# Raw dt as an outer product on TensorE; one more accumulating DMA for the state sums, and the skip term, gate and out-projection of a tile in parts

## The chip, the cores and the metric

One NeuronCore of a Trainium2 chip runs the whole program. The metric is device time in microseconds; of the kernel before there are three timed runs: 2022.76, 2023.56 and 2023.82 us (median 2023.56). Each kernel also has one profiled execution.

## What is computed

One perceiver layer over 64 batches of 32 rows of width 512 (all fp32 unless said): cross attention to 257 keys per batch with 16 heads, then a Mamba block, then a feed-forward net with quantised inputs and weights, each added to its input. The part that the change touches is the Mamba block (1024 inner channels, 16 states):

```
bcd = einsum('ble,ep->blp', x_, x_proj_w)             # B, C and one raw dt per row
dt  = softplus(bcd[..., -1:] * dt_w + dt_b)           # 1024 channels from one number per row
h_t = exp(dt*A) * h_(t-1) + (dt * x_) * B             # scan over the 32 rows of a batch
y   = sum over 16 states (h_t * C) + x_ * D           # D: the skip term
y   = y * silu(z);  out = y @ out_proj_w              # gate and out-projection
```

## The kernel before

The 2048 rows are 16 tiles of 128 rows (4 batches each). Channels lie on the partitions: 8 chunks `c` of 128 channels, so `dt`, `u`, `xs`, `zs`, `xD` are 128 x 8 x 128. PE, ACT, DVE, POOL and SP each run one instruction stream, written out by hand in `schedule` in one common order; semaphores connect them. `interval(ta, tm, to, more)` handles at once tile `ta` in attention, tile `tm = ta-1` in the first part of Mamba and tile `to = ta-2` in its second part. It has four steps, b = 0 to 3, one batch of attention each. Intervals 3 to 14 are one loop; 0, 1, 2 and 15 are written apart, and `tail` finishes the last two tiles. The feed-forward net follows.

What each step does on each engine, around the change:

- PE starts a step with `scores` (L1025, into banks 2 to 5) of a batch, then turns the next batch's context (L958), makes its keys (`kv_keys`, L992, banks 6 and 7, halves j = 0 and 1), transposes the softmax (L1034), makes values (L1003) and weighs them (L1045, bank 4). In b = 0 it also turns the normalised tile (L1092) and makes its first in-projection (L1099); in b = 1 it makes `bcd` (L1126), broadcasts the dt row over the partitions (L1134), makes the gate's in-projection (L1099) and the out-projection of tile `to` (`mamba_out`, L1140, bank 5).
- DVE takes the scores from the banks in four passes (`score_pass`, L1697) for a batch. In b = 0 this is preceded by `x1_write` (L1724), the attention's result; its layer norm (statistics on DVE, L1598 and L1603; rstd on POOL, L1498 to L1503; rows on ACT, L1304) leads to PE's L1092. Between these stand the steps of the state scan: `CHAIN` is a list of (chunk, op) with op 0 the product u*B (L1815), op 1 the scan (L1820), op 2 the product with C (L1826), op 3 the sum over 16 states (`last_sum`, L1792 and L1797). `BEGIN` and `FINISH` say at which place of a step which entries of `CHAIN` stand, for tile `tm` and tile `to`.
- For op 3, POOL's DMA (L1545) first adds states 8 to 15 onto 0 to 7 in memory, for every chunk but the last one (`whole(c)`), for which DVE does this level too (128x1024).
- `mamba_steps` (L1764): DVE makes the raw dt of the 8 chunks from the broadcast row by eight multiply-adds. `mamba_softplus` on ACT: Abs, Exp (both 128x1024), Ln in halves (L1415 to L1420). `mamba_dt` (L1770): DVE makes max(dt, 0) + ln(...) in halves. `mamba_u` (L1782): u = dt*xs in halves. `decays` (L1443): ACT makes exp(dt*A), eight instructions for half a chunk.
- `mamba_gated` (L1896, L1899): DVE adds the skip term `xD` and multiplies with the gate, each over all 8 chunks, in b = 1 after the last sum of tile `to`; then `mamba_u` of tile `tm` may write `u`, and PE's `mamba_out` starts.
- POOL also scales the mask for each batch (L1517) and copies x1 to x2 (`mamba_keep`, L1576, end of b = 3), which `x1_write` of the next interval waits for.

Of the kernel before, what the change touches and what calls it, by code (L numbers as in the profile page):

```python
# [39 lines left out]
def perceiver_kernel(nc, x, ctx_kv, mask, Wq, bq, Wk, bk, Wv, bv, Wo, bo, Win, conv_w, conv_b, Wx,  # L40
# [13 lines left out]
    with ExitStack() as ctx:  # L54
# [35 lines left out]
        chan = sb("chan", [P, 4, IC])  # L90
# [167 lines left out]
        bc_loaded = [sem("b_loaded"), sem("c_loaded")]  # L258
        dt_step = sem("dt_step")
# [4 lines left out]
        hb_added = [sem("hb_added0"), sem("hb_added1")]  # L264
        sum_step = sem("sum_step")
# [64 lines left out]
        DONE = {step: k + 1 for k, step in enumerate(CHAIN)}  # L330
        FINISH = {(0, "a"): range(21, 22), (0, "b"): range(22, 26), (0, "c"): range(26, 28),
                  (1, "a"): range(28, 29), (1, "t"): range(29, 31), (1, "p"): range(31, 32)}
        BEGIN = {(1, "w"): range(0, 1), (1, "d"): range(1, 3), (1, "e"): range(3, 4), (2, "a"): range(4, 5),
# [15 lines left out]
        def tail(part):  # L349
# [31 lines left out]
            part.mamba_steps(LAST)  # L381
# [55 lines left out]
        def schedule(part, engine):  # L437
# [22 lines left out]
            def interval(ta, tm, to, more):  # L460

                here, front, back = ta is not None, tm is not None, to is not None
                for b in range(BT):
# [57 lines left out]
                    if b == 1 and front:  # L521
                        part.rows_load(tm, 0)
                        part.mamba_steps(tm)
# [9 lines left out]
                    if following and b == 0:  # L533
                        part.kv_values(g + 1, 0, range(0, 2))
                    if here:
                        part.normalise(g)
# [21 lines left out]
                    if b == 1 and front:  # L558
                        part.mamba_softplus(tm)
                        part.mamba_gate(tm, keys)  # L560
                        part.mamba_dt(tm)
                    place("b")
# [24 lines left out]
                    if b == 1 and back:  # L587
                        part.mamba_gated(to)
                    if b == 1 and front:
                        part.mamba_u(tm)  # L590
                    if here:
                        part.weigh_values(g, ta, b)
# [38 lines left out]
        class Part:  # L631
# [33 lines left out]
            def weigh_values(self, g, t, b): pass  # L665
# [17 lines left out]
            def mamba_steps(self, t): pass  # L683
            def mamba_softplus(self, t): pass
            def mamba_dt(self, t): pass
            def mamba_u(self, t): pass
# [3 lines left out]
            def mamba_gated(self, t): pass  # L690
# [56 lines left out]
        def whole(c):  # L747
            return c == IC - 1

# [4 lines left out]
        BQKV_DMAS, EARLY_DMAS, OTHER_DMAS = 9, 2, 9  # L754
# [3 lines left out]
        def _(sp):  # L758
# [128 lines left out]
            def rest_of_setup():  # L887
                sp.dma_start(bo_sb[:], bo.partition_broadcast(P)).then_inc(early_loaded, 16)
                sp.dma_start(idb[:], ident_b).then_inc(w_loaded, 16)
                with nc.allow_non_contiguous_dma(reason="small vectors, once"):  # L890
                    sp.dma_start(convw[:], conv_w.rearrange("(c p) o k -> p c (o k)", p=P)).then_inc(w_loaded, 16)
                    for i, v in enumerate((conv_b, dt_w, dt_b, Dskip)):
                        sp.dma_start(chan[:, i, :], v.rearrange("(c p) -> p c", p=P)).then_inc(w_loaded, 16)
                    sp.dma_start(wo_sb[:], Wo.rearrange("(c p) n -> p c n", p=P)).then_inc(wo_loaded, 16)
# [37 lines left out]
        def _(pe):  # L932
# [10 lines left out]
            class Products(Part):  # L943
# [25 lines left out]
                def kv_keys(self, g, b, ta, tm, to, more):  # L969
# [5 lines left out]
                    for j in range(2):  # L975
                        if b == 0 and j == 0 and to is not None:
# [60 lines left out]
                def weigh_values(self, g, t, b):  # L1037
# [1011 lines left out]
```

## Time and profile before

| | us |
|---|---|
| median of 3 timed runs | 2023.56 |
| the profiled execution's own time | 2018.77 |
| its span, first to last instruction | 2017.0 |
| PE busy | 1853.5 (92%) |
| DVE busy | 1851.5 (92%) |
| ACT busy | 1622.9 (80%) |
| POOL busy | 493.6 (24%) |

The page gives the share of each engine over the whole span. In its 40 slices DVE stands at 9 tenths from slice 4 to slice 38, PE nearly so from slice 2 to slice 34. An engine's wait is put down to what released it; idle time is in square brackets in the timelines. Matmul records carry their latency, so the distance from one start to the next says what a group takes.

### The profile page before, as it was taken

Reading aid. Unit: us, or ns where it says so; the run is one execution under the profiler, and the core shown is the slowest. Engines: PE = TensorE matmul, PEld = TensorE weight load, DVE = VectorE, ACT = ScalarE, POOL = GpSimd, SP = SyncE. Lnnn points to the kernel's source line nnn. Section 1 sums busy time; section 2 is a strip of 40 time slices with the busy share of each in tenths; the row PEclk is TensorE's granted clock in tenths of the full one; section 3 lists DMA queues with packets and bytes.
Section 4 is the critical chain, followed back from the end, with each engine's and each line's share of the span. In section 5 each row is a group of like instructions: output and inputs, shape, how many; then the busy total and the mean of one; then the engine's idle time right before and its main releaser. Section 6 shows DMA issues by size and latency. Waiting matters only on the chain. (4 is left out here: it accounts for less than half of the span.)

```text
span 2017.0 us, 43545 instructions
## 1 busy us (share of the span) xinstructions
PE 1853.5 (92%) x14733; PEld 1275.4 (63%) x14748; DVE 1851.5 (92%) x2320; ACT 1622.9 (80%) x4425; POOL 493.6 (24%) x392
## 2 busy tenths in 40 slices
PE   7998998999999999999999999999998999567899
PEld 5576666756575766666676767666666657366444
DVE  1647999999999999999999999999999999999788
ACT  3458888898988889898889788888988888867483
POOL 1001214131414232241413141422314131201013
PEclk9999999999999999999999999999999999789899
DMA  9623333333433333343333334343333333420214
GB/s 300 218 77 95 85 95 85 93 80 85 86 105 74 97 80 75 93 94 90 82 95 80 86 74 115 66 93 87 77 95 85 93 79 91 94 85 11 74 45 143
DMA packets 93456, 189.54 MB, mean 94 GB/s; under 512 B 18768, under 2 KB 39904, under 8 KB 88160
## 3 DMA queue, kind: packets, MB, share of 16 engines
q1 hardware_dynamic: 78448, 133.32, 21.0%
q0 software_dynamic: 14832, 54.01, 14.5%
q8 instruction: 94, 1.54, 0.3%
q14 instruction: 82, 0.67, 0.1%
HBM read 116.12 MB, written 17.18 MB: 66 GB/s over the span
## 5 line engine op out<-in xcount | busy, mean ns | idle before, releaser
L1443 ACT ACTIVATE dA<-dt,A_sb 128x124 f32<-128x124 f32 x2048 | 618.0, 397 | 12.5 <-DVE dt L1770 12.4
L1820 DVE TENSOR_TENSOR_SCAN hb<-dA,hb 128x2048 f32<-128x2048 f32 x118 | 522.4, 4427 | 8.1 <-ACT dA L1443 4.3
L992 PE MATMUL bank<-ctxT,wk_sb 128*128 128x256 f32 x2048 | 466.5, 384 | 30.4 <-ACT Q L1329 19.6
L1003 PE MATMUL bank<-wv_sb,ctxT 128*128 128x512 f32 x1024 | 476.7, 607 | 2.3 <-ACT ctxT L1262 2.3
L992 PEld LDWEIGHTS bank<-ctxT,wk_sb 128*128 128x128 f32 x2048 | 382.1, 191 | 99.7 <-ACT Q L1329 25.3
L1003 PEld LDWEIGHTS bank<-wv_sb,ctxT 128*128 128x128 f32 x1024 | 189.0, 193 | 194.9 <-issue 189.5
L1545 POOL DMA_DIRECT2D hb<-hb x103 | 93.5, 908 | 858.9 <-DVE hb L1826 843.6
L1815 DVE TENSOR_TENSOR hb<-u,BC 128x2048 f32<-128x2048 f32 x118 | 270.4, 2291 | 5.7 <-DVE u L1782 2.6
L1826 DVE TENSOR_TENSOR hb<-hb,BC 128x2048 f32<-128x2048 f32 x117 | 268.9, 2298 | 1.5
L1099 PE MATMUL bank<-xn2T,win_sb 128*128 128x128 f32 x2048 | 239.0, 278 | 0.7 <-ACT xn2T L1358 0.7
L1099 PEld LDWEIGHTS bank<-xn2T,win_sb 128*128 128x128 f32 x2048 | 236.4, 195 | 4.2 <-issue 2.2
L1517 POOL TENSOR_SCALAR maskn<-maskb 128x257 f32<-128x257 f32 x64 | 137.6, 2150 | 260.8 <-DVE soft L1697 258.4
L1299 ACT ACTIVATE Pr<-Pr,soft 128x257 f32<-128x257 f32 x256 | 127.4, 506 | 56.7 <-DVE soft L1697 56.7
L1792 DVE TENSOR_TENSOR hb<-hb 128x512 f32<-128x512 f32 (+2 forms) x248 | 149.6, 603 | 5.0 <-DMA hb<-hb 0.5
L1336 ACT ACTIVATE Pr<-Pr,soft 128x256 f32<-128x256 f32 x256 | 109.0, 503 | 23.6 <-DVE soft L1710 23.6
L1278 ACT ACTIVATE KT<-bank,bqkv 128x256 f32<-128x256 f32 x256 | 105.6, 464 | 26.3 <-PE bank L992 26.2
L1262 ACT ACTIVATE ctxT<-bank,lastT 128x256 f32<-128x256 f32 x256 | 102.5, 479 | 27.8 <-PE bank L958 25.6
L1285 ACT COPY V<-bank 128x512 f32<-128x512 f32 x128 | 74.7, 583 | 58.2 <-PE bank L1003 29.1
L1756 DVE SCALAR_TENSOR_TENSOR xs<-xpad,convw,xs 128x128 f32<-128x128 f32 x384 | 103.7, 347 | 14.9 <-ACT xs L1377 14.4
L1140 PE MATMUL bank<-wout_sb,zs 128*128 128x512 f32 x240 | 106.9, 598 | 0.0
L1034 PE MATMUL bank<-idf,Pr 128*128 128x128 f32 x512 | 79.5, 285 | 29.7 <-ACT Pr L1336 26.7
L1697 DVE CUSTOM_DVE_ANT_0 Pr<-bank,maskn 128x257 f32<-128x257 f32 x256 | 93.1, 421 | 10.8 <-PE bank L1025 10.8
(167 smaller groups left out, 2434.0 us busy)
## 6 DMA issues: line engine op xcount, KB each, us to landing
hb<-hb POOLq DMA_DIRECT2D x103, 512.0 KB, 5.2
ctx_sb<-in_ctx_dram SPq DMA_DIRECT2D x64, 512.0 KB, 4.0
BC<-bcd_dram SPq DMA_DIRECT2D x32, 1024.0 KB, 7.2
maskb<-in_mask_Bx1x1xS_fk_dram SPq DMA_DIRECT2D x64, 128.5 KB, 3.3
wstage<-in_L_ffn_w_dram SPq DMA_DIRECT2D x4, 2048.0 KB, 11.3
x_sb<-in_x_dram SPq DMA_DIRECT2D x16, 256.0 KB, 3.7
win_sb<-in_L_attn_in_proj_w_dram SPq DMA_DIRECT2D x1, 4096.0 KB, 25.1
bo_sb<-bias_dram SPq DMA_DIRECT2D x64, 64.0 KB, 2.0
```

The source lines that it names most:

```text
L992: last = pe.matmul(bank[6 + j][:, (m % 2) * KF:(m % 2 + 1) * KF], wk_sb[:, c, m * P:(m + 1) * P], ctxT[:, c, :], start=(c == 0), stop=(c = ...
L1003: last = pe.matmul(bank[h][:], ctxT[:, c, h * P:(h + 1) * P], wv_sb[:, c, :], start=(c == 0), stop=(c == DC - 1))
L1099: last = pe.matmul(bank[6 + q % 2][:, e * P:(e + 1) * P], win_sb[:, c, n:n + P], xn2T[:, c, :], start=(c == 0), stop=(c == DC - 1))
L1140: last = pe.matmul(bank[5][:], zs[:, c, :], wout_sb[:, c, :], start=(c == 0), stop=(c == IC - 1))
L1299: act.activation(Pr[:, m, :], Pr[:, m, :], ACT.Exp, scale=-1.0, bias=soft[:, 0, m:m + 1], accum_out=soft[:, 1, m:m + 1]).then_inc(exp_done, 1)
L1336: act.mul(Pr[:, m, 0:KF], Pr[:, m, 0:KF], soft[:, 2, m:m + 1]).then_inc(p_ready, 1)
L1443: last = act.activation(dA[:, c % 2, n * BT:(n + 1) * BT, 1:], dt[:, c, :].rearrange("p (b s) -> p b s", s=S)[:, :, 1:], ACT.Exp, scale=A_ ...
L1517: pool.tensor_scalar(maskn[:], maskb[:], -NEG, 1.0, ALU.mult, ALU.mult).then_inc(mask_scaled, 1)
L1792: dve.tensor_tensor(tile[:, 0:n, :], tile[:, 0:n, :], tile[:, n:2 * n, :], ALU.add).then_inc(sum_step, 1)
L1815: ins = dve.tensor_tensor(tile, u[:, c, :].unsqueeze(1).broadcast_to([P, NS, P]), BC[:, 0:NS, :], ALU.mult)
L1820: ins = dve.tensor_tensor_scan(flat, dA[:, c % 2].rearrange("p n s -> p (n s)"), flat, 0.0, ALU.mult, ALU.add)
L1826: ins = dve.tensor_tensor(tile, tile, BC[:, NS:2 * NS, :], ALU.mult)
```

## The change

1. `dt_product` on PE takes the place of `mamba_steps` on DVE. `dt_w` and `dt_b` lie as rows in the new tile `dt_rows`, for channels 0 to 511 on partitions 0 and 1 and for the others on 32 and 33. `dt_row` on ACT makes of the broadcast row, with a scale and a bias per partition, the raw row on partitions 0, 32, ... and ones on 1, 33, .... Eight matmuls that contract over two partitions, alternating between the two groups of partitions and between banks 4 and 5, give the raw dt of all 1024 channels. They stand in `kv_keys` of b = 1 between its two halves, after the wait for DVE's score passes (which free the banks).
2. ACT's Abs reads the banks in two halves of 128x512, and Abs and Exp move forward to a `mamba_magnitude` ahead of `normalise`; `mamba_dt` reads the banks; `weigh_values` on PE in b = 1 waits for it.
3. The accumulating DMA does the first level for chunk 7 too. Two further ones per tile add `xD` onto `u` for chunks 0 to 3 (after the sum of chunk 3) and for 4 and 5 (after that of chunk 5).
4. `mamba_gated` is in halves: the first (chunks 0 to 3) and the first half of `mamba_u` stand right behind `mamba_dt`, and `CHAIN`'s entry (0, 0) of tile `tm` moves from place "w" to place "b", ahead of chunk 7's sum; the second half adds `xD` for chunks 6 and 7 only. `mamba_out` starts on its first four chunks when they are ready.
5. In the tail `gate_kept` adds `xD` for chunk 4 only, and `dt_product` and `mamba_magnitude` take the place of `mamba_steps`.

```diff
+                        if b == 1 and j == 1 and tm is not None:
+                            pe.wait_ge(scored, DC * g)
+                            self.dt_product(tm)
...
+                def dt_product(self, t):
+                    pe.wait_ge(dtrow_copied, t + 1)
...
+                    for k in range(DC):
+                        for r in range(2):
+                            rows = slice(r * DEPTH, r * DEPTH + 2)
+                            last = pe.matmul(bank[4 + r][:, k * P:(k + 1) * P], dt_rows[rows, k, :], BC[rows, 2 * NS, :],
+                                             start=True, stop=True)
+                    last.then_inc(dt_psum, 1)
...
-                    act.copy(BC[:, 2 * NS, :], bank[7][:, 0:P]).then_inc(dtrow_copied, 1)
+                    act.activation(BC[:, 2 * NS, :], bank[7][:, 0:P], ACT.Identity, scale=consts[:, 1:2],
+                                   bias=consts[:, 2:3]).then_inc(dtrow_copied, 1)
...
-                    for c in range(IC):
-                        dve.tensor_scalar(dt[:, c, :], BC[:, 2 * NS, :], chan[:, 1, c:c + 1], chan[:, 2, c:c + 1],
-                                          ALU.mult, ALU.add).then_inc(dt_step, 1)
...
+                    act.wait_ge(dt_psum, t + 1)
+                    for i in range(2):
+                        part = soft_tmp[:, DC * i:DC * (i + 1), :].rearrange("p c q -> p (c q)")
+                        last = act.activation(part, bank[4 + i][:], ACT.Abs)
...
+                        if op == 3 and c in (3, 5):
+                            i, first = (0, 0) if c == 3 else (1, 4)
+                            pool.wait_ge(scan_step, 4 * IC * t + k + 1)
+                            pool.wait_ge(xsD_ready, t + 1)
+                            pool.dma_start(u[:, first:c + 1, :], xD[:, first:c + 1, :], accum_op=ALU.add
+                                           ).then_inc(skip_added[i], 16)
...
+                    if b == 1 and back:
+                        part.mamba_gated(to, 0)
+                    if b == 1 and front:
+                        part.mamba_u(tm, (0,))
                     place("b")
...
-                dve.tensor_tensor(u[:], u[:], xD[:], ALU.add).then_inc(y_step, 1)
+                        dve.tensor_tensor(u[:, 6:8, :], u[:, 6:8, :], xD[:, 6:8, :], ALU.add).then_inc(y_step, 1)
+                    dve.tensor_tensor(zs[:, half, :], u[:, half, :], zs[:, half, :], ALU.mult).then_inc(y_ready, 1)
```

## Rows read from the trace of the kernel before

**Rows 1.** The page: engines' busy us (share of the span) x instructions.
```profile
span 2017.0 us, 43545 instructions
PE 1853.5 (92%) x14733; PEld 1275.4 (63%) x14748; DVE 1851.5 (92%) x2320; ACT 1622.9 (80%) x4425; POOL 493.6 (24%) x392
```
**Rows 2.** Busy time by stretch: first the columns; one interval, then two parts of it.
```profile
core 0: us, PE busy (x) PEld busy (x) DVE busy (x) ACT busy (x) POOL busy (x), PEclk, DMA share, GB/s
933.50:1043.10 109.60, 104.90 (x855) 72.39 (x855) 107.32 (x133) 94.92 (x270) 31.00 (x24) 0.98 0.36 87
...
894.67:944.45 49.78, 49.77 (x447) 35.75 (x448) 48.44 (x73) 41.57 (x105) 4.39 (x6) 1.00 0.30 86
...
954.70:958.20 3.50, 3.50 (x9) 1.86 (x8) 3.40 (x4) 3.50 (x12) 0.94 (x1) 0.54 0.54 102
```
**Rows 3.** Timeline of DVE: start us, us, instruction, count [idle before].
```profile
886.79 0.67 DVE L1724 TENSOR_TENSOR x<-bank,xbo 128x512 f32<-128x512 f32 x1
...
919.73 2.12 DVE L1764 TENSOR_SCALAR dt<-BC,chan 128x128 f32<-128x128 f32 x8
921.76 2.29 DVE L1826 TENSOR_TENSOR hb<-hb,BC 128x2048 f32<-128x2048 f32 x1
923.96 1.14 DVE L1792 TENSOR_TENSOR hb<-hb 128x512 f32<-128x512 f32 x2
...
926.55 2.40 DVE L1792 TENSOR_TENSOR hb<-hb 128x1024 f32<-128x1024 f32 x3
...
929.32 1.23 DVE L1896 TENSOR_TENSOR u<-u,xD 128x1024 f32<-128x1024 f32 x1
...
932.00 1.29 DVE L1782 TENSOR_TENSOR u<-dt,xs 128x512 f32<-128x512 f32 x2 [0.20 <-DVE zs L1899]
...
946.40 0.42 DVE L1697 CUSTOM_DVE_ANT_0 Pr<-bank,maskn 128x257 f32<-128x257 f32 x1
...
996.42 0.67 DVE L1724 TENSOR_TENSOR x<-bank,xbo 128x512 f32<-128x512 f32 x1
```
**Rows 4.** Timeline of PE, the same columns.
```profile
894.67 0.63 PE L1092 MATMUL bank<-idf,ln_out 128*128 128x128 f32 x4 [1.72 <-ACT ln_out L1304]
...
905.18 0.76 PE L1045 MATMUL bank<-PT,V 128*32 128x32 f32 x64
...
909.94 0.71 PE L1025 MATMUL bank<-KT,Q 32*32 32x257 f32 x32
...
920.55 7.31 PE L1099 MATMUL bank<-xn2T,win_sb 128*128 128x128 f32 x64
...
943.73 0.72 PE L1025 MATMUL bank<-KT,Q 32*32 32x257 f32 x32
```
**Rows 5.** Timelines of DVE and PE where DVE waits for the scores.
```profile
34.70 0.43 DVE L1697 CUSTOM_DVE_ANT_0 Pr<-bank,maskn 128x257 f32<-128x257 f32 x1 [0.61 <-PE bank L1025]
...
33.70 0.73 PE L1025 MATMUL bank<-KT,Q 32*32 32x257 f32 x32 [1.32 <-ACT Q L1329]
```
**Rows 6.** Timeline of ACT in b = 1.
```profile
924.34 1.15 ACT L1420 ACTIVATE xpad<-xpad 128x512 f32<-128x512 f32 x2
...
929.42 2.42 ACT L1443 ACTIVATE dA<-dt,A_sb 128x124 f32<-128x124 f32 x8
```
**Rows 7.** POOL's accumulating DMAs: one issue in the timeline; time to landing of all 103.
```profile
1003.24 0.95 POOL L1545 DMA_DIRECT2D hb<-hb  x1
...
DMA to landing us min/median/max: 4.5/5.2/10.3
```
**Rows 8.** Timelines at the ends of the loop: interval 1, interval 15, the tail.
```profile
169.16 4.42 DVE L1820 TENSOR_TENSOR_SCAN hb<-dA,hb 128x2048 f32<-128x2048 f32 x1 [2.62 <-ACT dA L1443]
...
1712.92 0.71 PE L1025 MATMUL bank<-KT,Q 32*32 32x257 f32 x32
...
1714.39 0.42 DVE L1697 CUSTOM_DVE_ANT_0 Pr<-bank,maskn 128x257 f32<-128x257 f32 x1
...
1800.56 1.28 DVE L1770 SCALAR_TENSOR_TENSOR dt<-dt,xpad 128x512 f32<-128x512 f32 x2
```

More of the change, by code:

```diff
@@ L380, in tail @@
             part.rows_load(LAST, 0)
-            part.mamba_steps(LAST)
+            part.dt_product(LAST)
+            part.mamba_magnitude(LAST)
             part.mamba_softplus(LAST)
@@ L534, in interval @@
                         part.kv_values(g + 1, 0, range(0, 2))
+                    if b == 1 and front:
+                        part.mamba_magnitude(tm)
                     if here:
@@ L561, in interval @@
                         part.mamba_dt(tm)
+                    if b == 1 and back:
+                        part.mamba_gated(to, 0)
+                    if b == 1 and front:
+                        part.mamba_u(tm, (0,))
                     place("b")
@@ L682, in dt_row, with dt_product, mamba_magnitude, mamba_u @@
             def dt_row(self, t, keys): pass
-            def mamba_steps(self, t): pass
+            def dt_product(self, t): pass
+            def mamba_magnitude(self, t): pass
             def mamba_softplus(self, t): pass
             def mamba_dt(self, t): pass
-            def mamba_u(self, t): pass
+            def mamba_u(self, t, halves=(0, 1)): pass
             def mamba_skip(self, t): pass
@@ L689, in scans, with mamba_gated @@
             def scans(self, t, steps): pass
-            def mamba_gated(self, t): pass
+            def mamba_gated(self, t, i): pass
             def kept_sum(self, t): pass
@@ L1040, in weigh_values @@
                     pe.wait_ge(pt1_copied, g + 1)
+                    if b == 1 and tm is not None:
+                        pe.wait_ge(dt_step, 2 * (tm + 1))
                     for m in range(DC):
@@ L1551, in mamba_pad @@
                         return
-                    wait(pool, dt_step, 10 * t)
+                    wait(pool, dt_step, 2 * t)
                     apart(pool)
@@ L1776, in mamba_u @@
                         dve.wait_ge(tail_fed, item(PREV, IC - 1))
-                    else:
-                        wait(dve, y_ready, t)
-                    for i, half in enumerate((slice(0, IC // 2), slice(IC // 2, IC))):
-                        dve.wait_ge(dt_step, 10 * t + 9 + i)
+                    for i in halves:
+                        half = slice(IC // 2 * i, IC // 2 * (i + 1))
+                        if not (isinstance(t, int) and t == LAST):
+                            wait(dve, y_ready, 2 * t - 1 + i)
+                        dve.wait_ge(dt_step, 2 * t + 1 + i)
                         dve.wait_ge(xs_ready, t + 1)
```

105 lines of the change are left out of this document (62 added, 43 removed).

## Prediction

> **What bounds the kernel now.** I read the page first [rows 1]: PE and DVE are both busy for 92% of the span, so the average says nothing on which of them sets the time. Then one interval of the loop [rows 2]: 109.60 us, of which DVE is busy for 107.32 and PE for 104.90. The rest of DVE's time is small gaps of dependent instructions, as the 0.20 us before the u products [rows 3]. So today DVE sets the period, and a reader who stops here will expect each microsecond taken from DVE to come back fourteen times.
>
> The timelines say how near the next limit is. Follow one loop through both engines [rows 3, 4]:
> - DVE writes x1 at 886.79. Through statistics, rstd and rows this becomes PE's transposes at 894.67, 7.88 us later; PE had waited 1.72 us for them, so this link is live.
> - From 894.67 to the end of the scores of step b = 2 at 944.45 (943.73 + 0.72), PE is busy for 49.77 of 49.78 us at a granted clock of 1.00 [rows 2]. No slack at all is in this stretch.
> - DVE takes these scores at 946.40. Where DVE is idle and waiting, its first pass starts 0.27 us after the end of PE's scores (34.43 to 34.70 [rows 5]). So it is late by 1.95 - 0.29 = 1.66 us here (I take 0.29 us as the floor; the handful of such waits lie between 0.27 and 0.30).
> - From 946.40 DVE works to the next x1 at 996.42, 50.02 us, and the loop is closed.
>
> Sum: 7.88 + 49.78 + 0.29 + 50.02 = 107.97 us, against a period of 109.63. All twelve intervals of the loop have 1.92 to 1.97 us between the scores and the pass at this place, so the 1.66 is the same everywhere. Whatever is put on PE between 894.67 and 944.45 eats into it. The new product is put exactly there.
>
> **What goes from DVE.** All in step b = 1, between DVE's passes of b = 1 and those of b = 2 [rows 3]:
> - eight multiply-adds: 921.76 - 919.73 = 2.03 us
> - the 128x1024 level of chunk 7: three levels and passes take 2.40 us where two take 1.14: 1.26 us
> - the skip term: 1.23 us for eight chunks; with two chunks left, by the slope between this row and the 0.65 us of a half (128x512) in the u products, some 0.4: 0.8 us
> - the gate in halves: twice 0.65 for 1.23, 0.1 us back, and two more dependent pairs at 0.20: 0.3 to 0.4 us back.
>
> Net 3.7 us per interval. New waits take some of it again. The raw dt is there later relative to DVE (below), so `mamba_dt` waits some 0.3 us for Ln; and the second half of chunk 0's decays (2.42 us [rows 6]) stands on ACT behind copies of the transposed softmax, which PE makes later by the price of the product, so the scan of chunk 0 waits some 0.5 us. Chunk 7's sum waits for its DMA: about 0.6 us until POOL issues plus 5.2 us to landing [rows 7] from the end of op 2. In between DVE has 1.4 (sum of chunk 6), 1.3 (dt), 0.65 and 0.65 (half gate, half u) and 2.3 (product of chunk 0), with two small gaps 6.7 us, against 5.8 to 7 with the load of the C rows, which starts at the same moment. Without that cover each microsecond would be DVE's; but there is a second cover: PE's out-projection of tile `to` ends about 941, and DVE's sum out of bank 5 waits for it, so up to 2 us of all this costs nothing.
>
> DVE would thus be ready for the passes of b = 2 at 945.0 (PE's out-projection, then 1.7 us of sum and statistics, then 2.2 us of product) where it was at 946.40.
>
> **What comes to PE.** Eight products, two records each. Its price D is what decides. A 128*128 product over 128 columns takes 7.31/64 = 0.114 us per record [rows 4], so 16 records one after another are 1.83 us. The trace has no product that contracts over two partitions. It has two groups in which the array is used in parts [rows 4]: the scores (32*32, sixteen parts; 32 records of 257 columns, 32 x 0.229 = 7.3 us one after another, 0.46 over sixteen parts) take 0.71 to 0.72 us; the weighing of values (128*32, four parts; 64 records of 32 columns, 1.82 us one after another, 0.46 over four) takes 0.76. Both fit "streams divided by the parts, plus 0.26 to 0.30". The new product has two parts (partitions 0 and 32, a bank each): 0.92 + 0.28, less some 0.05 by which these groups overlap the next: D = 1.15 us. Bounds: 0.3 (it fits into gaps) and 2.1 (no overlap of the parts, 1.83 + 0.28). I take the value nearest to the two groups in parts.
>
> The Trainium skill (TensorE: Matmul & The Clock Gate, Part 3, and its table of goals) says that a product over 32 partitions takes as long as one over 128 and gains only if others run in other row groups beside it; it gives 3.07x for four row groups. By that efficiency two groups would give 1.54x, and D = 1.2 plus the change of mode; if they ran apart, 1.83. No row here shows row groups alone.
>
> The wait for `scored` in front of the product costs nothing: DVE's passes of b = 1 end at 914.3 and PE comes there at 917. ACT's instructions are the same in sum (two Abs of a half each); keys' second copy, which PE needs for the second half of the gate's in-projection, comes by 922.9 and is needed at 925.3.
>
> **The sum.** PE reaches the end of the scores of b = 2 at 944.45 + 1.15 = 945.60, DVE starts at 945.89 instead of 946.40, and was ready at 945.0. The new period is 107.97 + 1.15 = 109.12: 0.51 us less, for 3.7 us taken from DVE.
> - 12 intervals: -6.1 us. Interval 2 has 1.70 where the others have 1.95: -0.3.
> - Interval 1 (no tile `to`): DVE waits 2.62 us for chunk 0's decays [rows 8], which stand behind the transposed softmax and so behind D: +1.15.
> - Interval 15: from 1713.63 to 1714.39 is 0.76 [rows 8], 0.47 over the floor: +0.7.
> - Tail: two waits go ahead of chunk 7's scan, but `mamba_dt` at 1800.56 [rows 8] stands behind the product (which waits for a sum on PE), two Abs, Exp and half of Ln: I find it within 0.4 us of where it is, and count 0 (bounds -1 and +1).
> - Setup: two DMAs more in number and one tiny reduction, hidden behind loads: 0.
>
> Together -4.6 us on a profiled time of 2018.77 (span 2017.0), which is 4.8 us under the median; on the median 2023.56 this gives 2019.0 us.
>
> POOL has three more issues of about 0.9 us per interval and is at 31 of 110 us [rows 2]. The two for the skip term land 20 us or more before they are needed. Behind the one after chunk 3 on POOL stands the copy of x1, now at about 990.4, which holds up one DVE instruction by 0.8 us as it does today, and which x1 at 996.42 waits for: 5 us of room. The skill (SBUF — State Buffer, the passage on the "DVE blocks DMA" trap) says that DVE instructions with two inputs in SBUF, or in a two-port mode, lock GpSimd out of a shared pair of ports, and that descriptors are then written late. The row speaks against it for these issues: the one at 1003.24 lies under DVE's 128x2048 product (1003.43 to 1005.7) and takes 0.95 us [rows 7] like the others. By the rule the copy would come after DVE's scan, x1 some 0.9 us late, and the sum would be +6.
>
> **Rivals.**
> - *The parts do not overlap* (17%). D = 2.1: the period is 0.45 over today's, 12 x 0.45 = 5.4, and 0.7, 2.1, 1.6 and 1 for interval 2, 1, 15 and the tail: +10.8, 2034 us. This is the slower side; it decides from D = 1.66. For it: only two rows of each part work, and no row shows the form. Against: both groups in parts fit one formula.
> - *The clock falls in the busy stretch* (6%). The granted clock is 0.54 for 3.5 us in b = 2 of this interval [rows 2], where it costs nothing since DVE is late there; in b = 1 it would cost 1.6 us of PE each time: 12 x 1.1 + 3, +16, 2040 us. For it: thin products are added. Against: 1.00 over all of the stretch.
> - *POOL is locked out* (4%): the +6 above, 2030 us, by an issue that waits for DVE's scan.
> - *DVE's own gain counts* (10%). If D is 0.3, PE is ready at 944.75 and DVE at about 945.0, and the period falls by 1.3: 12 x 1.3 + 1, -17, 2007 us.
> - *All of DVE's saving comes through* (5%): 14 x 3.7 = -52, 1972 us. It needs a PE that can be earlier at b = 2, which the 49.77 of 49.78 us exclude unless the order differs from what I read.
> - *Nothing to be seen* (13%): a wait of half a microsecond that I missed takes what is left, 2023 us.
>
> My forecast has 45%, 2015 to 2022 by itself. This kernel's measurements tell 0.2% (4 us) from no change. Faster by more: 0.33 of the forecast's share and the two on that side, 0.48. Within: 0.27 (the rest of the forecast's, nothing to be seen, and D just over 1.66). Slower: 0.25. The range, 2007 to 2034, leaves out the clock and the full saving.
>
> **What would show it.** The new product as 16 records in b = 1 that take about 1.1 us, start to start; DVE idle at the passes of b = 2 in every interval, released by PE's scores, 0.29 us after their end; a period of about 109.1; DVE busy per interval down by 3 to 4 us and almost none of it in the time; no wait at chunk 7's sum over 0.5 us; PE's wait before 894.67's transposes still there. It is wrong if DVE does not wait for the scores of b = 2, or if the product takes less than 0.8 or more than 1.7 us.

## The result, and the profile after

The changed kernel takes 2043.6 us (median of four runs, 2040.5 to 2045.9) against 2023.4 us of the kernel before on the same chip: ratio 1.0105, 95% interval 1.0093 to 1.0117. It is slower by 20 us; I had forecast 4.6 us faster, and 2043.6 lies above my range. The profiled execution has a span of 2038.6 us, 21.6 more than before [rows 1]:

```profile
span 2038.6 us, 44073 instructions
...
PE 1877.5 (92%) x14989; PEld 1298.0 (64%) x15004; DVE 1788.9 (88%) x2193; ACT 1624.1 (80%) x4441; POOL 544.1 (27%) x435
```

DVE lost 63 us of work and the kernel got slower: DVE is idle for 84 us more. The list of DVE's waits (what waits, for whom: us in total, times, longest) says where, the ones of the setup left out:

```profile
DVE hb L1838 <- DMA hb<-hb: 29.7, 14, 3.0
DVE Pr L1749 <- PE bank L1041: 23.2, 18, 6.4
...
DVE Pr L1749 <- issue: 15.5, 11, 1.9
...
DVE x L1957 <- PE bank L1171: 8.2, 13, 1.0
```

In the loop of the kernel before there was none of the four (its five waits for scores stand ahead of the loop). The third is not a wait for another engine. One interval on DVE, against [rows 3]:

```profile
784.70 0.66 DVE L1776 TENSOR_TENSOR x<-bank,xbo 128x512 f32<-128x512 f32 x1
786.66 0.43 DVE L1749 CUSTOM_DVE_ANT_0 Pr<-bank,maskn 128x257 f32<-128x257 f32 x1 [1.31 <-issue]
...
829.69 1.15 DVE L1838 TENSOR_TENSOR hb<-hb 128x512 f32<-128x512 f32 x2 [1.68 <-DMA hb<-hb]
...
840.89 0.69 DVE L1957 CUSTOM_DVE_ANT_0 x<-bank,x 128x512 f32<-128x512 f32 x1 [1.00 <-PE bank L1171]
...
845.41 0.43 DVE L1749 CUSTOM_DVE_ANT_0 Pr<-bank,maskn 128x257 f32<-128x257 f32 x1 [0.58 <-PE bank L1041]
...
894.89 0.66 DVE L1776 TENSOR_TENSOR x<-bank,xbo 128x512 f32<-128x512 f32 x1
```

Between x1 and the first pass of scores DVE issues nothing for 1.3 us. Before, the pass followed 0.58 us behind x1. This happens at 11 places, the 11 jumps from the end of the loop back to its start (idle for 1.04 to 1.90 us); in the intervals that are written apart it does not. PE in the same interval, against [rows 4]:

```profile
793.96 0.63 PE L1110 MATMUL bank<-idf,ln_out 128*128 128x128 f32 x4 [3.12 <-ACT ln_out L1337]
...
795.44 7.38 PE L1117 MATMUL bank<-xn2T,win_sb 128*128 128x128 f32 x64
...
816.58 1.16 PE L1163 MATMUL bank<-BC,dt_rows 2*128 2x128 f32 x16
817.67 3.72 PE L1008 MATMUL bank<-ctxT,wk_sb 128*128 128x256 f32 x16
...
844.40 0.72 PE L1041 MATMUL bank<-KT,Q 32*32 32x257 f32 x32
```

The new product is as forecast: 16 records, 1.09 us from start to start. DVE waits for the scores of b = 2 and starts 0.29 us after their end. But the transposes come 9.26 us after x1 instead of 7.88, and PE waits 3.12 us for them where it waited 1.72. In six of the intervals that has a second price. The stretches behind the transposes, first in the interval before this one, then in this one (columns as in [rows 2]):

```profile
682.45:692.58 10.13, 10.13 (x77) 10.13 (x78) 9.96 (x11) 7.68 (x23) 2.79 (x3) 0.83 0.42 92
793.96:802.66 8.70, 8.70 (x77) 8.52 (x77) 8.53 (x5) 7.68 (x23) 1.90 (x2) 1.00 0.49 107
```

The same work takes 10.13 us at a granted clock of 0.83 and 8.70 at 1.00: part of it ran at 1.2 instead of 2.4 GHz, behind a wait of 3.24 us. From the transposes to the end of the scores this makes 52.48 us instead of 51.07 to 51.16.

So at the 11 jumps the interval of 109.63 us became 109.9 to 110.4 or, with the lower clock, 111.3 to 112.1, mostly in turns. Over the profiled executions: the first x1 is 4.0 us later, the 15 intervals are 12.5 us longer, and what follows the last x1 is 5.1 us longer; together 21.6.

### The profile page after: what moved, and what is told of

The parts are those of the page before. It is cut to its first block and busy times, and to the rows that moved or that the text cites. A ratio compares the mean times of both kernels' runs of the same rounds, so it can differ in the third digit from the quotient of the medians.

```text
span 2038.6 us, 44073 instructions
## 1 busy us (share of the span) xinstructions
PE 1877.5 (92%) x14989; PEld 1298.0 (64%) x15004; DVE 1788.9 (88%) x2193; ACT 1624.1 (80%) x4441; POOL 544.1 (27%) x435
## 3 DMA queue, kind: packets, MB, share of 16 engines
q14 instruction: 137, 1.12, 0.2%
## 5 line engine op out<-in xcount | busy, mean ns | idle before, releaser
L1019 PE MATMUL bank<-wv_sb,ctxT 128*128 128x512 f32 x1024 | 469.9, 599 | 2.3 <-ACT ctxT L1295 2.3
L1594 POOL DMA_DIRECT2D hb<-hb x117 | 105.2, 899 | 822.8 <-DVE hb L1873 797.3
L1117 PEld LDWEIGHTS bank<-xn2T,win_sb 128*128 128x128 f32 x2048 | 241.2, 198 | 3.4 <-issue 1.3
L1332 ACT ACTIVATE Pr<-Pr,soft 128x257 f32<-128x257 f32 x256 | 127.1, 506 | 50.9 <-DVE soft L1749 50.9
L1838 DVE TENSOR_TENSOR hb<-hb 128x512 f32<-128x512 f32 x234 | 132.4, 566 | 33.8 <-DMA hb<-hb 29.7
L971 PEld LDWEIGHTS bank<-idf,ctx_sb 128*128 128x128 f32 x512 | 58.2, 144 | 63.7 <-issue 29.3
```

The costliest lines, as they stand in the source:

```text
L1019: last = pe.matmul(bank[h][:], ctxT[:, c, h * P:(h + 1) * P], wv_sb[:, c, :], start=(c == 0), stop=(c == DC - 1))
L1117: last = pe.matmul(bank[6 + q % 2][:, e * P:(e + 1) * P], win_sb[:, c, n:n + P], xn2T[:, c, :], start=(c == 0), stop=(c == DC - 1))
L1332: act.activation(Pr[:, m, :], Pr[:, m, :], ACT.Exp, scale=-1.0, bias=soft[:, 0, m:m + 1], accum_out=soft[:, 1, m:m + 1]).then_inc(exp_done, 1)
L1838: dve.tensor_tensor(tile[:, 0:n, :], tile[:, 0:n, :], tile[:, n:2 * n, :], ALU.add).then_inc(sum_step, 1)
```

## The experiments

"Interval" is the distance of x1 to x1 in undisturbed passes of the loop (rows not late, clock at 1.00); where such passes are few, a second value stands for the others; "jump" is by how much the first pass of scores comes later behind x1 than 0.58 us, at the 11 jumps; "fetches" counts the packets of 8 KB of the instruction queue q14 in the whole execution.

| run | kernel | median us | ratio, 95% interval | interval | jump | fetches |
|---|---|---|---|---|---|---|
| | before | 2022 to 2023 | 1 | 109.63 | 0 | 82 |
| | after | 2043.6 | 1.0093 to 1.0117 | 110.2 / 111.7 | 1.1 to 2.0 | 137 |
| e1 | after, 11 idle on DVE ahead of the loop | 2017.8 | 0.9967 to 0.9990 | 108.75 | 0 | 83 |
| e2 | before, 118 idle ahead | 2051.3 | 1.0117 to 1.0152 | 111.2 / 112.3 | 1.1 to 1.8 | 138 |
| e3 | before, 36 idle on PE in each pass | 2023.6 | 0.9995 to 1.0014 | 109.63 | 0 | 82 |
| e4 | after, rows for the product loaded later | 2039.4 | 1.0065 to 1.0099 | 110 to 113 | 1.2 to 2.4 | 137 |
| e5 | e1, product doubled | 2060.5 | 1.0164 to 1.0195 | 109.62, then 112.4 | 0 | 82 |
| e6 | e1, product cut to a quarter | 2012.1 | 0.9942 to 0.9973 | 108.05 | 0 | 82 |
| e7 | after without the product | 2021.3 | 0.9984 to 1.0002 | 109.25 | 0 | 82 |
| e8 | e1, a turn behind the scores | 2015.6 | 0.9952 to 0.9975 | 108.29 / 110.1 | 0 | 82 |
| e9 | e8, bias rows loaded earlier | **2007.7** | 0.9913 to 0.9941 | 108.28 | 0 | 82 |
| e10 | e7, DVE makes chunk 7's level | 2013.8 | 0.9939 to 0.9968 | 108.31 / 109.4 | 0 | 82 |
| e11 | after, 45 idle ahead | 2017.9 | 0.9956 to 0.9984 | 108.72 | 0 | 82 |
| e12 | e1, DVE makes chunk 7's level | 2020.6 | 0.9973 to 0.9994 | 108.73 | 0 | 82 |
| e13 | e1, 40 idle in the body | 2017.8 | 0.9965 to 0.9997 | 108.73 | 0 | 82 |
| e14 | after, 64 idle ahead | 2016.4 | 0.9932 to 1.0000 | 108.77 | 0 | 82 |
| e15 | e5, 40 idle on PE ahead | 2086.6 | 1.0275 to 1.0335 | 114 to 116 | 0 | 82 |
| e16 | after, 64 idle ahead, 60 in the body | 2024.1, one run | | 109.1 | 0 | 138 |

Theory A: DVE waits at the jump because the instructions at its target have to be fetched again, and whether they are held depends on where DVE's program lies. The change took 12 instructions from DVE ahead of the loop (451, now 439) and 8 out of its body (300, now 292; counts of the program, whose differences the traces show to within two).

**e1.** Eleven semaphore increments that nobody waits for, in DVE's part of the setup:

```diff
                 def load_rest(self):
                     dve.wait_ge(wq_scaled, DC + 1)
+                    for _ in range(11):
+                        apart(dve)
```

> The changed kernel with 11 idle semaphore increments on DVE ahead of the loop, in setup, where DVE waits for A_sb; nothing in the loop differs. Theory A (DVE waits for its own instructions): at each of the 11 jumps back in the loop DVE stands idle 1.1 to 2.0 us after x1_write with nothing that releases it, because its loop now lies one fetched block further than before (the changed kernel has 11 fewer instructions ahead of it); put back to its old place the waits go, 15.5 us in all, PE waits less for the layer norm and its clock stays up: 2043.6 - 15.5 - up to 8.5 = 2020 to 2028 us, and 5 instead of 11 fetches of 8 KB per interval. Theory B (the wait comes from DMA traffic or POOL's new issues): nothing changes, 2043 us.

Eleven instructions that do nothing make the kernel 25.8 us faster than the change alone, and faster than before. The timeline of DVE at a jump:

```profile
779.82 0.66 DVE L1778 TENSOR_TENSOR x<-bank,xbo 128x512 f32<-128x512 f32 x1
780.40 0.41 DVE L1751 CUSTOM_DVE_ANT_0 Pr<-bank,maskn 128x257 f32<-128x257 f32 x1
```

The pass follows at 0.58 us again, and in nine of the 11 intervals the transposes at 7.82 to 7.87 us. In the two profiled executions the intervals behind the 11 jumps take 1221.0 us together in the changed kernel and 1198.1 in e1. The later passes are 16.4 of this and the lower clock in six intervals 6 x 1.41 = 8.5; 2.1 go off for two intervals of e1 with late rows, one of them at a lower clock. The instruction queue of the changed kernel (packets, MB, share of the DMA engines):

```profile
q14 instruction: 137, 1.12, 0.2%
```

and of e1:

```profile
q14 instruction: 83, 0.67, 0.1%
```

54 packets are gone, about five for each of 11 jumps. One of them ends the wait. In the changed kernel the window from 784.4 to 785.0 us, around x1 at 784.70, holds one (packets, MB, share):

```profile
q14 instruction: 1, 0.01, 4.0%
```

It landed at 784.86, 1.80 us ahead of the pass at 786.66. In e1 the queue has none from 777.6 to 781 us, around its x1 at 779.82. At all 11 jumps of the changed kernel a packet lands 1.67 to 1.88 us ahead of the pass, though the idle time varies from 1.04 to 1.90 us: the wait ends at a nearly fixed distance behind the packet.

**e2.** The same into the kernel before, 118 increments.

```diff
                     dve.wait_ge(wq_scaled, DC + 1)
+                    for _ in range(118):
+                        apart(dve)
```

> The kernel before with 118 idle semaphore increments on DVE ahead of the loop, in setup, so that its loop lies where the changed kernel's does, counted modulo 128 instructions. Theory A: the wait after x1_write appears in the kernel before, 11 times 1.1 to 2 us: 2023.4 + 12 to 22 = 2035 to 2046 us. Theory B: 2023 us, within 3.

```profile
1011.68 0.67 DVE L1726 TENSOR_TENSOR x<-bank,xbo 128x512 f32<-128x512 f32 x1
1013.86 0.43 DVE L1699 CUSTOM_DVE_ANT_0 Pr<-bank,maskn 128x257 f32<-128x257 f32 x1 [1.51 <-issue]
```

A kernel in which nothing else is changed gets the same wait at the same 11 places, and loses 29 us. Here too a packet lands 1.68 to 1.88 us ahead of the pass each time (in e4 1.60 to 1.92), with 0.96 to 1.75 us of idle time. The loss is more than forecast since the clock follows: in nine intervals the stretch behind the transposes takes 50.9 to 51.3 us instead of 49.8. The wait thus needs neither the product nor the new DMAs.

**e3.** The same question for PE, in each pass of the kernel before, ahead of the wait for the normalised rows:

```diff
+                    if not isinstance(t, int):
+                        for _ in range(36):
+                            apart(pe)
                     pe.wait_ge(ln_done[1], t + 1)
```

> The kernel before with 36 idle semaphore increments on PE in each pass of the loop, ahead of the transposes that wait for the layer norm anyway (1.7 us of idle time). It lengthens PE's loop by as many instructions as the new product does. If PE's instruction fetches (16 KB each, none in some intervals of the kernel before, 10 in every interval of the changed one) cost time, this kernel has them in every interval and is 5 us or more slower; if they cost nothing by themselves, it stays within 3 us of 2023.

No difference in time, while the 16 KB packets of PE's instruction queue q8 went from 94 to 139, as many as the changed kernel has (140). So that number alone, which I had found beside the other, explains nothing.

**e4.** The four loads of `dt_rows` go behind the third load of a context, to see what the first x1's 4.0 us are:

```diff
                     sp.dma_start(maskb[:], mask_rows[g].partition_broadcast(P)).then_inc(mask_loaded, 16)
+                    if isinstance(g, int) and g == 2:
+                        for r in range(2):
+                            for i, v in enumerate((dt_w, dt_b)):
...
```

> The changed kernel with the four loads of dt_rows put behind the third context load in SP's queue. In the changed kernel that context lands 1.6 to 2.5 us later than before, PE waits 5.72 us for it where it was 3.24, and its clock is low afterwards; the first x1_write is 4.0 us later. Theory: the issue time of the loads in front of it does this; it comes back in part, 1 to 4 us: 2040 to 2043. Rival: the loads of the other small vectors, or chance in the queue, set it: no change.

The first x1 came at 124.0 us. But it came at 125.3 in e3, whose setup is that of the kernel before, at 125.9 in e2, which has the idle instructions besides, and at 122.8 to 126.9 in all the others. The 121.53 belongs to that one execution of the kernel before; the change is not shown to cost anything there. Against the changed kernel the run is 4 us faster with touching intervals (1.0065 to 1.0099 and 1.0093 to 1.0117), which I leave open.

**e5, e6: the price of the product.** In e5 it is issued twice; e6 leaves the raw dt of six chunks out in the loop.

```diff
-                    for k in range(DC):
+                    for k in (*range(DC), *range(DC)):                  # e5
+                    for k in range(DC if isinstance(t, int) else 1):    # e6
```

> The changed kernel with the 11 idle increments ahead of the loop (2017.8 us, loop period 108.75), and the eight outer products issued twice. Theory A (with DVE's wait at the jump gone, PE's scores of b = 2 set the period, and the product's price is the sum's term D): 16 more records cost 0.8 to 1.05 us in each of 13 intervals and the tail, period 109.6 to 109.8, DVE still waits 0.29 us after the scores of b = 2; 2028 to 2031 us. Rival (DVE or something else sets the period and the product lies beside it): 2018 us, and the margin at b = 2 shrinks elsewhere.

> The same with only two of the eight outer products in the 12 intervals of the loop; the raw dt of the other channels is left out there, so its output is not the layer's. Theory A: the product takes about 0.35 us instead of 1.1, the period falls from 108.75 to 108.0, which is still set by the scores of b = 2 (DVE stood idle there for 0.58 us and at the out-projection's sum for 0.68); 2018 - 12 x 0.75 = 2009 us. Rival (DVE is the limit as soon as the product is short): 2016 to 2018 us with a margin at b = 2 over 0.5 us.

From the transposes to the end of the scores of b = 2 it is 50.40 us with 4 records, 51.07 with 16, 51.96 with 32, and 49.78 without the product (e10): 0.056 us a record, half of the 0.114 of one after another, and some 0.4 for the switch. The two parts of the array do overlap. The interval follows nearly one for one: 108.05, 108.75, 109.62. That is the mechanism of the forecast. (e6 took 2012.1 us for 2009 expected; passes with late rows or a lower clock cost its profiled execution some 3 us.) But e5 took 2060 us, not 2030, since at the jumps PE now has a wait of its own:

```profile
674.98 0.73 PE L1041 MATMUL bank<-KT,Q 32*32 32x257 f32 x32 [0.32 <-issue]
675.64 0.77 PE L971 MATMUL bank<-idf,ctx_sb 128*128 128x128 f32 x5
679.53 0.90 PE L971 MATMUL bank<-idf,ctx_sb 128*128 128x128 f32 x3 [3.12 <-issue]
```

and in the list of PE's waits:

```profile
PE bank L971 <- issue: 33.9, 11, 3.6
```

Eleven times again, in the middle of a group of eight transposes, 33.9 us together. Each time a packet of 16 KB on PE's queue q8 lands 1.15 to 1.45 us ahead of the instruction that ends the wait, while the wait itself is 2.45 to 3.60 us long. Yet q8 moves 140 packets in e5 and 140 in e1, and e1 has one at this place too (it lands at 778.0, 1.8 us ahead of x1) without such a wait. So PE's waits too end behind a fetch, and it is not the number of fetches that brings them.

**e7, e10, e12: DVE's share and chunk 7's DMA.** e7 puts `mamba_steps` back in place of `dt_product`, with its Abs and Exp; e10 (from e7) and e12 (from e1) take the first level of chunk 7 back to DVE:

```diff
+                        part.mamba_steps(tm)                            # e7
-                            self.dt_product(tm)
...
-                        if op == 2:
+                        if op == 2 and c != IC - 1:
...
-                    n = NS // 4
+                    n = NS // 2 if c == IC - 1 else NS // 4
```

> The changed kernel without the outer product: DVE makes the raw dt by eight multiply-adds as before (Abs, Exp at their old place), everything else of the change stays (DMA for chunk 7, skip term by DMA, gate and out-projection in halves). Theory A: its DVE program starts the loop at another place, so the wait at the jump is absent (0.0 us after x1); PE's stretch to the scores of b = 2 is 49.8 us again; but DVE carries 2.03 us of multiply-adds and the 2.0 us wait for chunk 7's DMA, comes to b = 2 at 60.0 us after x1 and sets the period: 109.4 to 109.6, 2019 to 2023 us, the same as the kernel before. Rival (the DMA wait shrinks, and the 1.7 us taken from DVE count down to the floor at the scores): period 108.0, 2003 us. Second rival (the wait at the jump is a cost of the parts in DMA or halves, not of where the program lies): 2035 us or more.

> As e7 (no outer product, 2021.3 us, period 109.25, DVE ready for b = 2 last), and DVE again makes chunk 7's first level itself (128x1024) in place of the accumulating DMA, for which it waited 2.1 us in each interval. Theory A: without slack at b = 2 that wait was on the path: 2.10 - 1.26 = 0.84 us less per interval, period 108.4, 2021 - 13 x 0.84 = 2010 us. Rival (the wait was covered by PE's out-projection): period 109.2, 2021 us.

> As e1 (the changed kernel with 11 idle increments, 2017.8 us), and DVE again makes chunk 7's first level itself. DVE waited 2.0 us for that DMA in each interval, and then stood idle for 0.68 us at the out-projection and 0.58 us at the scores of b = 2. Theory A: the wait lies beside PE's work; 2.0 - 1.26 = 0.7 us less for DVE only lengthen its waits for PE, period 108.75, 2016 to 2019 us. Rival (the DMA's wait is on the path): 2018 - 13 x 0.7 = 2009 us.

Without the product DVE comes last, and its wait for chunk 7's DMA counts: 109.25 us with it, 108.31 without (0.94 less, 0.84 expected). With the product, DVE's wait for the out-projection takes its place and the interval stays at 108.73. (e10's 2013.8 for 2010 and e12's 2020.6 for 2016 to 2019 lie a little above what was expected: in nine and five of their twelve intervals of the loop the rows are late by 0.3 us or more.) The row of that wait in e1:

```profile
DVE x L1959 <- PE bank L1171: 8.4, 13, 1.1
```

and in e12:

```profile
DVE x L1960 <- PE bank L1171: 20.2, 14, 1.6
```

e7 as a whole is no faster than the kernel before: all that was moved off DVE bought nothing but room for a DMA's wait, until that DMA is taken out too.

**e8, e9: what comes next.** In e8 PE turns the first half of the next context behind the scores of b = 2 instead of ahead. In e9 the bias rows of a tile are loaded at the end of b = 3 of the interval before.

```diff
-                    if following and 0 < b < BT - 1:                    # e8, at both places
+                    if following and b == 1:
...
+                    if b == 3 and here and more and not (isinstance(ta, int) and ta == 0):
+                        part.load_bias(ta + 1)                          # e9
                     if b == 3 and front:
                         part.mamba_keep(tm)
```

> The changed kernel with the 11 idle increments, and in b = 2 PE turns the first half of the next context behind the scores instead of ahead of them. Theory A: the stretch from the transposes of the normalised tile to the end of the scores of b = 2 falls from 51.07 to 50.54 us, DVE (idle there for 0.58 us) starts 0.53 us earlier, period 108.2; 2018 - 12 x 0.53 = 2011 to 2012 us. Rival (what is moved behind comes back, since b = 3 or the values wait for it): no change, 2018 us.

> As e8 (11 idle increments, the first half of the context turned behind the scores in b = 2; 2015.6 us, period 108.29 with six of twelve intervals at 110), and the bias rows are loaded at the end of b = 3 of the interval before instead of after x1. In e8 POOL's sum with them started 2.1 us after x1, as soon as they had landed, which made the layer norm's rows 0.3 us late in half of the intervals and 3.5 us late in interval 15, and the granted clock fell behind PE's wait for them. Theory A: POOL's sum starts 0.6 us after x1, x1 to the transposes is 7.87 us everywhere, fewer intervals lose 1.4 us to the clock, and interval 15 gets its 1.5 to 5 us back: 2005 to 2010 us. Rival (the clock falls behind PE's wait of 1.7 us anyway): 2013 to 2015 us.

e8's interval fell by 0.46 us, yet the kernel by only 2.2. Four intervals of its loop (not six, as the expectation of e9 says) and interval 15 took 110. In them, on POOL and on PE:

```profile
778.49 1.28 POOL L1573 TENSOR_TENSOR xbo<-x_sb,bo_sb 128x512 f32<-128x512 f32 x1 [6.25 <-DMA bo_sb<-bias_dram]
779.75 2.34 POOL L1540 TENSOR_SCALAR stats<-stats 128x1 f32<-128x1 f32 x1
...
784.62 0.63 PE L1110 MATMUL bank<-idf,ln_out 128*128 128x128 f32 x4 [2.03 <-ACT ln_out L1337]
...
786.57 8.34 PE L1117 MATMUL bank<-xn2T,win_sb 128*128 128x128 f32 x64
```

The sum with the bias rows starts 2.05 us after x1, when they land, and pushes the layer norm's rows 0.3 us back; the products after them take 8.34 us instead of 7.38. In e9:

```profile
884.59 1.28 POOL L1576 TENSOR_TENSOR xbo<-x_sb,bo_sb 128x512 f32<-128x512 f32 x1 [5.19 <-DVE x L1781]
...
891.48 0.63 PE L1113 MATMUL bank<-idf,ln_out 128*128 128x128 f32 x4 [1.68 <-ACT ln_out L1340]
```

It starts 1.0 us after x1, released by x1 itself; the clock stays at 1.00 behind the transposes, and all 12 intervals of the loop take 108.28 to 108.45. With 2007.7 us this is the fastest kernel of the study, 36 us under the changed kernel and 0.73% under the one before.

**e11, e13, e14, e16: what decides on DVE's wait.** 45 (e11) and 64 (e14, e16) increments ahead of the loop of the changed kernel, and increments in the body ahead of chunk 7's sum, where DVE stood idle:

```diff
                 def last_sum(self, t, c):
                     tile = hb[:, c % 2]
+                    if c == IC - 1 and not isinstance(t, int):
+                        for _ in range(40):                             # e13; 60 in e16
+                            apart(dve)
```

> The changed kernel with 45 idle increments on DVE ahead of the loop instead of 11; the loop's body has the same 292 instructions. Ahead of the loop stand 439 in the changed kernel (waits at every jump), 450 in e1 (none), 451 before (none), 569 in e2 (waits), 456 in e7 (none). Theory A1 (what counts is how many aligned blocks of 64 instructions the loop covers: six, and it is fetched anew in each pass; five, and it isn't): 484 to 776 covers six, so the waits of 1.1 to 2.0 us and 11 fetches per interval come back, 2035 to 2044 us. Rival A2 (the place of the jump's target in its block counts: it was at 55 and 57 where the waits were, at 2, 3 and 8 where not; here it is at 36): 2017 to 2020 us.

> As e1 (11 idle increments ahead of the loop: the jump's target where it doesn't wait), and 40 idle increments more inside the loop's body, ahead of DVE's 2.0 us wait for chunk 7's DMA, where they are hidden: 332 instructions instead of 292. Theory A1 (the loop is held if it covers few enough blocks, and fetched anew in each pass if not): 11 instead of 5 fetches of 8 KB per pass; with the target where it was the jump's wait may come back too: then 2035 us. Rival A2 (only the target's place decides on the wait): fetches may rise, but 0.0 us after x1, and 2016 to 2020 us.

> The changed kernel with 64 idle increments ahead of the loop, so that 503 instructions stand there instead of 439. If the blocks that count are 64 of these instructions long, the loop lies in them as in the changed kernel: waits of 1.1 to 2.0 us at 11 jumps, 11 fetches per pass, 2038 to 2045 us. If they are 128 long, or the wait depends on something else (any added instruction ahead of the loop removes it): none, 2016 to 2020 us.

> The changed kernel with 64 idle increments on DVE ahead of the loop and 60 in its body, ahead of the wait for chunk 7's DMA: 503 to 855. If a block holds 128 of these instructions and one begins at about 449, the target lies 54 behind a block's start and the loop covers four blocks, as in the changed kernel, where e14 covered three. Theory A1 (four blocks: fetched anew in each pass): about 10 fetches of 8 KB per pass instead of 5, but next to no wait after x1, since the block's end follows 74 instructions behind the target; 2015 to 2022 us. Rival A2 (only a target close to a block's end makes fetches): 5 fetches per pass, the same time.

A1 as it stood fell with e11, and blocks of 64 instructions with e14. Put together: 439 and 569 instructions ahead of the loop wait, 450, 451, 456, 484 and 503 do not; the two that do are 130 apart. This fits blocks of 128 instructions of which one begins at about 449. The loop then covers three blocks in before, e1, e7, e11, e13 and e14 (82 or 83 packets), and four in after, e2 and e16 (137 or 138): no run contradicts. The 332 instructions in the body of e13 change neither the packets nor the wait. e16 covers four with the target far from a block's end, and there the two things part: the 138 packets are back, but not the wait. I take it that the missing block is needed only later; no run shows that by itself. Its DVE timeline at a jump:

```profile
784.24 0.66 DVE L1778 TENSOR_TENSOR x<-bank,xbo 128x512 f32<-128x512 f32 x1
784.83 0.41 DVE L1751 CUSTOM_DVE_ANT_0 Pr<-bank,maskn 128x257 f32<-128x257 f32 x1
```

(Its 2024 us, above the range expected, are partly the 60 increments themselves, 3.8 us in each pass, more than the gap they stand in.)

**e15.** The same for PE: e5 with 40 increments ahead of the loop.

```diff
                 def last_values(self):
+                    for _ in range(40):
+                        apart(pe)
                     pe.wait_ge(scored, DC)
```

> As e5 (outer products issued twice, 2060 us, PE idle for 3.1 us at the first instructions of 11 passes), with 40 idle increments on PE ahead of the loop. Theory: PE's wait is of the same kind as DVE's and hangs on where its loop lies; here it is gone or moved behind other work, the period is 109.6 to 109.7 in every interval, and 2028 to 2033 us are left for the doubled product, as was forecast for e5. Rival (the wait comes from the longer body or from the doubled product itself): 2055 to 2061 us.

The wait is not gone, as I had expected, but moved, and grew:

```profile
682.98 0.67 PE L1043 MATMUL bank<-KT,Q 32*32 32x257 f32 x18
687.17 1.10 PE L1043 MATMUL bank<-KT,Q 32*32 32x257 f32 x14 [3.51 <-issue]
```

In e5 it stood after 32 + 5 matmul records of the pass, here after 18: 19 records, each with its weight load, so 38 instructions earlier for 40 put ahead. The place of the wait is fixed in the program, not in the work; again a 16 KB packet lands 1.27 to 1.65 us ahead of its end. What stays open: why PE's wait is next to absent with the single product (0.3 to 0.6 us, a handful of times), and so whether the doubled one's place or its length brings it.

## Why the prediction was wrong, point by point

- *The step that failed* is the first term of my sum, the 7.88 us from x1 to the transposes, which I carried over unchanged. It became 9.0 to 9.8 us at the 11 jumps. Nothing that the change does stands in that stretch, and I treated what it does not touch as fixed; the change had shifted the program under it. e1 takes this alone away and gives 2017.8 us, for 2019.0 forecast; against its own runs of before it is faster by 0.22%, where I had 0.23%. e2 gives the wait to the old kernel and makes it slower by 29 us.
- *That e1 meets the forecast so closely is partly luck.* In the profiled executions its 12 intervals of the loop are 10.8 us shorter than those of the kernel before, where I had 6.1, and its interval 15 is 6.0 us longer, where I had 0.7. There the bias rows landed late: POOL's sum started 3.5 us after x1 and PE's transposes came 11.4 us after it, for 7.7 in the kernel before, with the lower clock behind them:

```profile
1661.35 1.12 PE L1110 MATMUL bank<-idf,ln_out 128*128 128x128 f32 x4 [5.25 <-ACT ln_out L1337]
```

Why the bias rows land later in some executions than in others is not shown.
- The Trainium skill has the rule, in Runtime: NRT & Kernel Launch, Instruction fetch mechanics: fetching runs ahead in sequence, and a taken branch to a target outside what is held "forces a DMA fetch of the target page before execution can continue". I did not weigh it. The traces agree in kind (e1, e2, e16); they show packets of 8 KB on DVE's queue where the page has 16 KiB blocks for every engine.
- *The clock.* My rival said that it falls within the busy stretch of b = 1 by the new thin products, and priced that at 2040 us. The time came out near that, the cause did not: it falls behind PE's longer wait for the rows, in b = 0, and in e2 without any product. The trace of the kernel before had one such interval, which the prediction does not mention: PE waited 2.49 us instead of 1.72, and the stretch behind took 51.18 us at a granted clock of 0.97 instead of 49.78 at 1.00.

```profile
1114.16 0.63 PE L1092 MATMUL bank<-idf,ln_out 128*128 128x128 f32 x4 [2.49 <-ACT ln_out L1304]
...
1114.16:1165.34 51.18, 51.17 (x447) 37.35 (x448) 48.77 (x73) 41.57 (x105) 4.00 (x8) 0.97 0.32 85
```

- *The product's price D*, 1.15 us: measured 1.09 from start to start and 1.29 in the stretch (51.07 - 49.78). The overlap of the parts held and the fixed part was 0.4 instead of 0.23. By the Trainium skill (TensorE: Matmul & The Clock Gate, Part 3) I had an estimate of 1.2 plus the change of mode, which comes out as near.
- *From DVE's pass to x1*, carried over as 50.02: it is 49.49. POOL's copy of x1, now behind one more DMA issue, no longer meets the short sum (0.29 instead of 1.12 us) and costs the scan 0.29 (4.71 instead of 4.42 us). These 0.53 less and D's 0.14 more make the interval 108.75 for 109.12.
- *Chunk 7's wait*, "no wait over 0.5": 1.65 to 2.4 us in the loop and 3.0 in interval 15. The DMA lands 7.7 us after its issue at 821.95, where I had taken 5.2 with 5.8 to 7 for all. The cover that I named, the out-projection, holds it (e12), and e10 shows its price where it does not.
- *POOL's DMA issues are not locked out, but its copy of x1 is held up.* The new issue at 773.42 in e1 lies under DVE's 128x2048 product (772.85 to 775.1) and takes 0.85 us. The copy behind it starts under the same product and takes 1.66 us, for 0.93 in the kernel before, where it ends ahead of one:

```profile
988.63 0.93 POOL L1576 COPY x<-x 128x512 f32<-128x512 f32 x1
...
773.96 1.66 POOL L1625 COPY x<-x 128x512 f32<-128x512 f32 x1
```

In all 15 passes of the changed kernel, and in the one pass of the kernel before where the copy starts under the product (there it takes 2.31 us), it ends 0.47 us behind the product's end. It costs the 0.29 us of scan named above; x1 comes 4.2 us behind it and does not wait for it, so the +6 of the rival does not come. I had read the page of the Trainium skill too widely (SBUF — State Buffer): its passage on the trap speaks of the two-port mode alone, and its section Who interferes with whom names two SBUF inputs only against a GpSimd instruction that reads SBUF. The copy is such an instruction, and the traces agree.
- *The tail*, counted 0 with bounds of -1 and 1: in the profiled execution `mamba_dt` of the last tile comes 37.7 us after the last x1 instead of 35.8, with a wait of 2.7 for Ln. But with the same wait it comes after 35.7 in e4 and 35.9 in e14, so the 1.9 us are not shown to be the change's. Nor are the 5.1 us of the whole tail: e2's, an unchanged program, was 5.6 us longer than that of the kernel before, and e1's, with the change, 1.7.
- *DVE is ready before the scores of b = 2* in every interval of the loop, waits 0.58 us and starts 0.29 us behind their end: right.

## What to carry to other kernels

When a change adds or removes instructions of an engine with a loop, look at that engine's first instructions after the jump back: idle time put down to "issue" there, once per pass, and more packets on the instruction queue are a cost of where the program lies, and a few idle instructions ahead of the loop move it. Test for it before the change itself is judged; here it was worth 26 us, more than all the rest of the change. And a stretch that no edit touches is still a term to be bounded: for 1.5 us of wait on DVE this kernel paid another 1.4 in every second interval through the clock.

## What the runs showed of the hardware that I had not expected

- DVE idle for 1.0 to 2.3 us at a taken jump (after, e2, e4), with about five more packets of 8 KB per pass, where 439 or 569 instructions stand ahead of the loop; 0.0 us with 450 to 503. In all 33 cases the wait ends 1.6 to 1.9 us behind the landing of a packet. PE idle for 2.5 to 4.3 us (e5, e15), which ends 1.2 to 1.7 us behind a packet of 16 KB in all 22 cases.
- Two row groups that contract over two partitions each run beside one another: 0.056 us per record of 128 columns.
- The granted clock fell behind waits of 2.0 us (e8) and 3.2 us (after), and did not behind one of 3.12 us in the next interval (after), nor behind one of 3.57 us (e2); with 1.5 to 1.9 us in each interval (e9) the loop ran at 1.00 there. The traces do not tell more.
- A POOL instruction on 128 numbers (L1540) took 0.23 us, and 2.34 us in e8, where it began under DVE's 128x2048 product; POOL's copy of 128x512 took 0.93 us, and 1.65 to 2.31 us under one.
